# Decoder layer on one core: later key stacks by a ScalarE copy and GpSimd head products, rope partly on GpSimd, two head groups per output bank

## The chip, the cores and the metric

One core of a Trainium2 chip runs the whole kernel. The metric is the device time of one execution in microseconds. TensorE does the matmuls (its records are called PE, its weight loads PEld), VectorE is DVE, ScalarE is ACT, GpSimd is POOL, and SyncE (SP) issues DMAs.

## What is computed

A decoder layer with the norms behind the residuals, for x of 2 x 512 x 128 and a context of 2 x 154 x 128, all in fp32:

```python
x = layernorm(x + self_attention(x))       # 16 heads of 8; causal
x = layernorm(x + cross_attention(x, ctx)) # 16 heads of 8; keys 154
x = layernorm(x + ffn(x))                  # 8 experts of 256, the best 2 of each token

# self attention
q = rope(x @ wq.T); k = rope(x @ wk.T); v = rope(x @ wv.T)
qh, kh, vh = q @ wqi.T + bqi, k @ wki.T + bki, v @ wvi.T + bvi
attn = softmax(where(causal, qh @ kh.T / sqrt(8), -inf))
out = (attn @ vh) @ out_w.T + out_b
```

The ffn is silu(h1) * h3 through w2 for every expert, weighted by the router.

## The kernel before

The layout is transposed: channels on the 128 partitions, 512 tokens in the free dimension. The 16 heads go in NG = 4 groups of G = 4, one head to each 32 partitions. A **unit** u is one stage (0 self, 1 cross), one batch and one group: NU = 16 units, of which the first 8 are self attention.

The steps, by the names that the planner's items have:

- `U` (b, w), w one of q, k, v: x times wq, wk or wv (L748), then VectorE multiplies the bank by the cosine and the sine table into `ab` (L1142, L1144). That is the rope; its swap of neighbours is in the weights of the next step.
- `H` (b, w): projection of q or k by four fp32 records (L755, L756). ScalarE rounds it to `high` (L990), VectorE writes the rest to `low` (L1150). `VH` is the same for v (L766), written to `v_sb` (L1183), which has 32 columns for each head: 8 of v, a one for the sum, zeros.
- `SQ`, `SK` (b, g): 0/1 matrices `fr` select a group's rows from high and low into one bank (L725, L726), so that each head's 32 partitions hold the parts of q or k. `fr` is made by ScalarE from loaded constants (`FR`, L980 four times and L981). ScalarE copies q to `qa`. The key **stack** `kst` of a unit has a block of 512 columns for each head and zeros on the other heads' partitions: ScalarE writes the blocks of heads 0 and 1 (L1010, 32 partitions each), VectorE those of heads 2 and 3 (L1165), into tiles that were cleared at the start. `SC` does so for the context's keys, `kc` (L1018, L1173).
- `A` (u, k): scores by query rows (L812), 11 banks a unit in self attention, 6 in cross attention. VectorE takes the negative row maximum of each head (L1230, L1235).
- `MP` (u): GpSimd writes the 16 maxima, rounded, and their rests to `mpad` (L666, L667). `MT` (u): TensorE adds them to q by a matmul with the identity (L822, L824); ScalarE copies the result to `qb`.
- `B` (u, k): scores by key rows (L840), ScalarE's Exp to `prob` (heads 0, 1) and `prob_more` (L1047). `MK`: GpSimd zeroes above the diagonal (L675, two instructions for each of four key tiles).
- `PV` (u, kt): v times probabilities, four heads at once, each on 32 columns of the array (L857; in cross attention L865, L868). The key tiles 0, 1, 3, 2 are items of their own.
- `POC` (u): ScalarE copies the output bank `psO`, of which there is one, so PV of unit u + 1 waits for it. `OT` (u): four transposes (L876), VectorE divides by the sums (L1246, L1247). After four groups `ONT`, `OP` (output projection), `LN`, `LNX`.
- `XB`: GpSimd adds a bias to the loaded x_tok (L638). `F1`, `F3`, `F2`: the experts (L719 to L721, L947), two loops of 16 tiles.

PSUM's eight banks are rings: `psA` 3, `psB` 2, `psO` 1, `psJ` 2 for everything else (`J`). All engines run fixed lists of items in the order that `schedule` writes: a list scheduler over `tasks()`, which gives every item its stages (engine, microseconds), the items it waits for, and rings. It starts what can start first, and among equals what has the longest way to the end. At run time each engine goes through its list in order and waits on semaphores.

Loads are issued at the start by SP and by ScalarE, one (`brow`, the bias rows) by GpSimd.

Of the kernel before, what the change touches and what calls it, by code (L numbers as in the profile page):

```python
# [43 lines left out]
C_CQ = C_ONE + 4  # L44
# [13 lines left out]

SIZE = {"A": 3, "B": 2, "O": 1, "J": 2}
Y_AFTER = (NU - NG - 2 if SIZE["O"] == 2 else NU - 1, NU - 1)  # L60
# [42 lines left out]
def po_bank(u):  # L103
    return u % 2 if u < NU - NG and SIZE["O"] == 2 else SIZE["O"] - 1


def po_back(u):

    return 2 if u < NU - NG and SIZE["O"] == 2 else 1
# [9 lines left out]

def part_users(n):  # L120

    key = [k for k, v in PART.items() if v == n][0]
    if key == ("c",):
        return [("SC", (g,)) for g in range(NG)]
    if key[0] == "k":
        return [("SK", (key[1], g)) for g in range(NG)]
    return [("SQ", (int(key[0] == "x"), key[1], g)) for g in range(NG)]
# [4 lines left out]
    "J": {"U": (1, 1), "H": (1, 2), "VH": (1, 1), "SQ": (1, 1), "SK": (1, (1, 2)), "SC": (1, (1, 2)), "CK": (2, 1), "CV": (1, 1),  # L132
# [5 lines left out]
LATENCY = {"PE": 0.22, "ACT": 0.17, "DVE": 0.15, "POOL": 0.18, "SP": 0.1, "LOAD": 0.1}  # L138


def tasks():
# [16 lines left out]
    dve = lambda n: 0.065 + n / 958.0  # L158
    act = lambda n: 0.12 + n / 1390.0
    mm = lambda n: max(0.137, n / 2300.0)  # L160
# [3 lines left out]
    add("LOAD", (0,), [("LOAD", 6.5)])  # L164
    add("LOAD", (1,), [("LOAD", 1.0)])
    add("LOAD", (2,), [("LOAD", 1.5)])
    add("LOAD", (3,), [("LOAD", 6.0)])
    add("FR", (), [("ACT", 2.4)], [("LOAD", (2,))])
    for b in range(B):
        for n, w in enumerate("qkv"):  # L170
            late = []
            if 3 * b + n >= 2:
                m = 3 * b + n - 2
                late.append((1, ((("H", (m // 3, "qk"[m % 3])) if m % 3 < 2 else ("VH", (m // 3,))), 0)))
            add("U", (b, w), [("PE", 0.86), ("DVE", 1.2)], [("LOAD", (b,))], late)
# [21 lines left out]
    for u in range(NU):  # L197
        st, b, g = unit(u)
        fills = a_fills(u)
        for k, parts in enumerate(fills):  # L200
# [3 lines left out]
            deps = [("SQ", (st, b, g)), ("SK", (b, g)) if st == 0 else ("SC", (g,))] if k == 0 else []  # L204
# [4 lines left out]
        add("MP", (u,), [("POOL", 0.5)], [("A", (u, len(fills) - 1))] + ([(("MT", (u - 2,)), 0)] if u >= 2 else []))  # L209
        add("MT", (u,), [("PE", 0.78), ("ACT", 0.5)], [("MP", (u,))],  # L210
            [(1, (("B", (u - 2, len(b_fills(u - 2)) - 1)), 0))] if u >= 2 else [])
        for k, blocks in enumerate(b_fills(u)):
            widths = [S - 128 * kt if st == 0 else S for kt, _, _ in blocks]
            deps = [("MT", (u,))] + ([("KT", ())] if st == 1 and k == NG else [])
            late = [(1, ("PV", (u - 2, 2 if unit(u - 2)[0] == 0 else 1)))] if u >= 2 and k == 0 else []
            add("B", (u, k), [("PE", sum(mm(w) for w in widths)), ("ACT", act(sum(widths)))], deps, late)
        if st == 0:
            for kt in (0, 1, 3, 2):
                add("MK", (u, kt), [("POOL", 0.72)], [("B", (u, exps_of(u, kt)[-1]))])
            pv = [(kt, us, [("MK", (u, kt)), ("VH", (b,))]) for kt, us in ((0, 0.86), (1, 0.65), (3, 0.22), (2, 0.43))]  # L220
# [1201 lines left out]
```

## Time and profile before

| | us |
|---|---|
| runs | 289.09, 289.03, 287.84; median 289.03 |
| the profiled execution | 290.4 |
| its span, first to last instruction | 288.3 |
| PE, DVE, ACT, POOL busy | 262.7, 203.1, 155.9, 110.8 |
| mean granted TensorE clock | 0.975 |

The span is about 2 us shorter than the execution's own time. "Busy" is the time that an engine's instructions cover. Matmuls overlap and their ends are modelled, so a stretch in which PE is always busy can still hold small waits. Clock 1.00 is 2.4 GHz, 0.50 is 1.2 GHz.

### The profile page before, as it was taken

The page shows a single profiled execution, that of the slowest core. Times are in us where ns is not written, and L with a number is a line of the kernel's source. Part 1 is how long each engine was busy: PE and PEld are TensorE (multiplying, and loading weights), DVE is VectorE, ACT ScalarE, POOL GpSimd, SP SyncE. Part 2 cuts the span into 40 slices and gives each one's busy share as a digit, 9 for nine tenths or more (in the row PEclk, how much of TensorE's full clock was granted, in tenths as well). Part 3 has the DMA queues.
Part 4 walks back from the last instruction along what each step waited for, and adds up shares of the span by engine and source line. Part 5 has one row for each costly group of instructions (what it writes and reads, how often), then busy time and mean ns, then how long its engine had stood idle before and what let it go on. Part 6 is the DMA issues. An engine that isn't in the chain of part 4 may idle for free.

```text
span 288.3 us, 4324 instructions
## 1 busy us (share of the span) xinstructions
PE 262.7 (91%) x1326; PEld 161.2 (56%) x1326; DVE 203.1 (70%) x603; ACT 155.9 (54%) x293; POOL 110.8 (38%) x175
## 2 busy tenths in 40 slices
PE   6478799999999899999999989999989999999980
PEld 2135656655655556667654666566656556565640
DVE  7639688897889988766573499835788854555464
ACT  1446135576789955867788747685342333432300
POOL 9950003413323353133743232025364455554531
PEclk9977799999999999999999999999999999999997
DMA  7920002000000400000212100000000000000002
GB/s 199 392 60 0 1 0 75 0 3 1 3 0 0 145 3 0 2 1 0 68 44 67 45 1 0 2 1 0 2 0 1 0 2 0 0 0 2 0 0 73
DMA packets 5797, 8.62 MB, mean 30 GB/s; under 512 B 720, under 2 KB 3280, under 8 KB 5648
## 3 DMA queue, kind: packets, MB, share of 16 engines
q1 hardware_dynamic: 4976, 7.14, 7.6%
q10 hardware_dynamic: 720, 0.95, 0.9%
q0 software_dynamic: 80, 0.26, 0.6%
q8 instruction: 11, 0.18, 0.3%
q14 instruction: 10, 0.08, 0.1%
HBM read 7.83 MB, written 0.52 MB: 29 GB/s over the span
## 4 chain that ended last, share of the span: by engine, by line
PE 76%; ACT 7%; DVE 7%; issue 3%; DMA 3%; POOL 2%; SPq 0%; POOLq 0%; DVEq 0%; ACTq 0%
PE psB L840 10%; PE psA L812 10%; PE psO L947 8%; PE psO L857 7%; PE psB L719 3%; PE psO L865 3%; DMA c<-c_dram 3%; PE psJ L876 2%; PE psO L868 2%; PE psA L720 2%; PE psA L721 2%; PE psA L719 2%; PE psB L721 2%; PE psB L720 2%; PE psJ L824 2%
## 5 line engine op out<-in xcount | busy, mean ns | idle before, releaser
L1230 DVE CUSTOM_DVE_ANT_0 junk<-psA,c 128x128 bf16<-128x128 f32 (+3 forms) x128 | 56.1, 486 | 5.8 <-PE psA L812 5.4
L690 POOL TENSOR_TENSOR gated<-silu,wbc 128x512 f32<-128x512 f32 x32 | 41.1, 1286 | 41.5 <-DVE hid L1344 30.1
L1047 ACT ACTIVATE prob<-psB 128x512 f32<-128x512 f32 (+1 forms) x88 | 47.6, 560 | 16.1 <-PE psB L840 15.0
L1101 ACT ACTIVATE silu<-psA 128x512 f32<-128x512 f32 x32 | 19.1, 598 | 44.6 <-PE psA L721 40.3
L1334 DVE SCALAR_TENSOR_TENSOR silu<-silu,psA 128x512 f32<-128x512 f32 x32 | 21.9, 684 | 27.8 <-ACT silu L1101 27.8
L812 PE MATMUL psA<-kst,qa 128*128 128x512 f32 (+1 forms) x88 | 39.8, 460 | 1.3 <-DVE kst L1165 1.2
L840 PE MATMUL psB<-qb,kst 128*128 128x512 f32 (+3 forms) x128 | 37.6, 337 | 1.0 <-ACT prob_more L1047 0.5
L1235 DVE TENSOR_REDUCE negm<-psA 128x3 f32<-128x462 f32 (+1 forms) x48 | 26.1, 579 | 10.3 <-PE psA L812 9.9
L947 PE MATMUL psO<-hid,w 128*128 128x512 f32 x64 | 33.1, 598 | 0.2 <-DVE hid L1344 0.2
L675 POOL TENSOR_SCALAR_AFFINE_SELECT prob<-prob 128x256 f32<-128x256 f32 x32 | 13.2, 413 | 50.3 <-ACT prob_more L1047 50.1
L1047 ACT ACTIVATE prob_more<-psB 128x512 f32<-128x512 f32 (+1 forms) x48 | 24.6, 530 | 12.1 <-PE psB L840 11.6
L840 PEld LDWEIGHTS psB<-qb,kst 128*128 128x128 f32 x128 | 22.6, 189 | 12.3 <-issue 5.2
L812 PEld LDWEIGHTS psA<-kst,qa 128*128 128x128 f32 x88 | 17.1, 195 | 15.8 <-issue 11.4
L1344 DVE TENSOR_TENSOR hid<-psB,gated 128x512 f32<-128x512 f32 x32 | 21.9, 686 | 3.4 <-PE psB L721 3.2
L857 PE MATMUL psO<-prob,v 128*32 128x512 f32 (+3 forms) x128 | 23.4, 445 | 1.0 <-POOL prob_more L675 1.0
L857 PE MATMUL psO<-prob_more,v 128*32 128x512 f32 (+3 forms) x128 | 23.4, 445 | 0.0
L719 PE MATMUL psA<-x_high,w1high 128*128 128x512 f32 x32 | 22.0, 687 | 0.0
L666 POOL CAST mpad<-negm 128x16 fp32r<-128x16 f32 x16 | 3.4, 212 | 44.0 <-DVE negm L1230 26.2
L812 PE MATMUL psA<-kc,qa 128*128 128x462 f32 (+2 forms) x64 | 18.5, 345 | 0.3 <-DVE negm L1235 0.2
L840 PE MATMUL psB<-qb,kc 128*128 128x512 f32 x32 | 15.6, 498 | 1.3 <-ACT prob L1047 0.9
L719 PE MATMUL psB<-x_high,w3high 128*128 128x512 f32 x32 | 16.5, 515 | 0.0
L725 PE MATMUL psJ<-high,fr 128*128 128x512 f32 (+1 forms) x28 | 13.0, 465 | 3.4 <-DVE kst L1165 2.1
(150 smaller groups left out, 522.9 us busy)
## 6 DMA issues: line engine op xcount, KB each, us to landing
c<-w_dram SPq DMA_DIRECT2D x8, 256.0 KB, 2.8
w<-w_dram SPq DMA_DIRECT2D x1, 1024.0 KB, 4.9
c<-c_dram SPq DMA_DIRECT2D x1, 666.0 KB, 9.4
xT<-xt_dram SPq DMA_DIRECT2D x2, 256.0 KB, 6.0
x_tok<-x_dram SPq DMA_DIRECT2D x1, 512.0 KB, 10.0
out_dram<-x_tok SPq DMA_DIRECT2D x2, 256.0 KB, 2.3
wa<-wa_dram ACTq DMA_DIRECT2D x2, 192.0 KB, 5.5
wx<-wx_dram SPq DMA_DIRECT2D x1, 384.0 KB, 8.6
```

The costliest lines, as they stand in the source:

```text
L690: nc.gpsimd.tensor_tensor(gated[:, n % 2, :], silu[:, n % 2, :], wbc[:, (E * b + f // 2) % 2, :], ALU.mult).then_inc(s_sg, 1)
L719: nc.tensor.matmul(ps[:, :], w_high[:, cols], x_high[:, b, :], start=True, stop=False)
L812: last = nc.tensor.matmul(ps[:, c:c + heads * width].rearrange("p (n w) -> p n w", n=heads), qa[:, u % SLOTS, 128 * i:128 * i + 128], keys ...
L840: last = nc.tensor.matmul(ps[:, c:c + S - 128 * kt], keys, qb[:, u % 2, 128 * kt:S], start=m == 0, stop=m == len(blocks) - 1, skip_group_c ...
L857: last = nc.tensor.matmul(po[32 * j:32 * j + 32, 128 * kt:S], v_sb[b][:, kt, G * g + j, :], prob_at(u, kt, j), start=kt == 0, stop=kt == 2 ...
L947: nc.tensor.matmul(psO[b % SIZE["O"]][:, :], w2[:, 128 * f:128 * f + 128], hid[:, n % 4, :], start=f == 0, stop=f == FT - 1).then_inc(s_y, 1)
L1047: nc.scalar.activation(dst, psB[n % SIZE["B"]][:, 0:cols], ACT.Exp, scale=SCALE).then_inc(b_done[n % SIZE["B"]], 1)
L1101: nc.scalar.activation(silu[:, n % 2, :], psA[a % SIZE["A"]][:, :], ACT.Tanh, scale=0.5).then_inc(s_th, 1)
L1230: last = nc.vector.tensor_tensor_reduce(out=junk[:, p, cols], in0=psA[p][:, cols], in1=c32[:, C_MASK + S - width:C_MASK + S], scale=-1.0, ...
L1235: last = nc.vector.tensor_reduce(negm[:, u % 2, :, :].rearrange("p i j -> p (i j)")[:, G * i + j:G * i + j + heads], psA[p][:, 0:heads * S ...
L1334: nc.vector.scalar_tensor_tensor(out=silu[:, n % 2, :], in0=silu[:, n % 2, :], scalar=1.0, in1=psA[a % SIZE["A"]][:, :], op0=ALU.add, op1= ...
L1344: nc.vector.tensor_tensor(hid[:, n % 4, :], psB[h % SIZE["B"]][:, :], gated[:, n % 2, :], ALU.mult).then_inc(b_done[h % SIZE["B"]], 1)
```

## The change

1. **Stacks.** Only unit 0 keeps the old way (now `SK0`). For the other seven, ScalarE copies the whole bank with its bias to a new tile `kcomp` (two buffers), which frees the bank, and GpSimd writes the four blocks of `kst`, each a product of kcomp over 128 partitions with a column `C_HEAD + j` that is 1 on head j's partitions and 0 elsewhere. Zeros are then written with the rest, so three of the four kst buffers and kc are no longer cleared. `SC` goes the same way (308 columns).
2. **Rope** of (0, v) and of batch 1: ScalarE copies the bank to `rest`, GpSimd makes both products. (0, q) and (0, k) stay on VectorE.
3. **MP** goes from GpSimd to VectorE, same two instructions.
4. **Output bank.** Units of even and odd g share one bank: v's 8 columns and the one now start at column 16 of each 32, and a group reads a window of 32 columns that begins at 16 (even g) or 0 (odd g), so that its results fall into the lower or upper half and zeros into the other. `POC` and `OT` are done once for two units, 8 times instead of 16.
5. **Bursts.** The PV items of self attention are two instead of four: key tile 0, then 1, 3 and 2 together.
6. **Loads and first items.** On SP: `wa` 7:10, `brow` and `c16` come in (c16 last), the selection constants go to ScalarE's queue. `FR` is five items, and a selection waits for its own group alone. U (0, v) waits for H (0, k), U of batch 1 for MT (0).
7. `onorm` lies in the constants' memory. The planner's latencies and costs have other numbers, which moves items on every engine.

```diff
+BURSTS = ((0,), (1, 3, 2)), ((0,), (1,))
+ROPE = {(b, w): "DVE" if (b, w) in ((0, "q"), (0, "k")) else "POOL" for b in range(B) for w in "qkv"}
+V_AT = 16
+def v_from(g):
+    return V_AT * (1 - g % 2)
...
-LATENCY = {"PE": 0.22, "ACT": 0.17, "DVE": 0.15, "POOL": 0.18, "SP": 0.1, "LOAD": 0.1}
+LATENCY = {"PE": 0.21, "ACT": 0.2, "DVE": 0.18, "POOL": 0.16, "SP": 0.1, "LOAD": 0.1}
...
+            if (b, w) == (0, "v"):
+                deps.append((("H", (0, "k")), 0))
+            if b:
+                deps.append((("MT", (0,)), 0))
...
-            act.dma_start(wa[:, 7:10, :], wa_d[:, 7:10, :]).then_inc(s_iv, 16)
-            act.dma_start(c16[:, :], c16_d).then_inc(s_c16, 16)
+            act.dma_start(c32[:, C_FR:C_MASK], c32_d[:, C_FR:C_MASK]).then_inc(s_fr, 16)
...
+                elif kind == "U":
...
+                    nc.gpsimd.tensor_tensor(ab[:, n % 2, 0, :], rest[:, m % 2, :], c32[:, C_CA:C_CA + S], ALU.mult)
+                    nc.gpsimd.tensor_tensor(ab[:, n % 2, 1, :], rest[:, m % 2, :], c32[:, C_SA:C_SA + S], ALU.mult).then_inc(s_rope, 1)
+                elif kind == "SK":
...
+                    for j in range(G):
+                        nc.gpsimd.tensor_scalar(kst[:, u % SLOTS, j, :], kcomp[:, u % 2, :], c32[:, C_HEAD + j:C_HEAD + j + 1], None,
+                                                ALU.mult).then_inc(s_km, 1)
...
-                    for j in (0, 1):
-                        rows = slice(32 * j, 32 * j + 32)
-                        last = nc.scalar.activation(kst[rows, u % SLOTS, j, :], ps[rows, :], ACT.Identity, bias=c32[rows, C_ONE:C_ONE + 1])
-                    free(JOB[item], last)
+                    if u >= 3:
+                        act.wait_ge(s_km, G * (u - 2))
+                    free(JOB[item], nc.scalar.activation(kcomp[:, u % 2, :], ps[:, :], ACT.Identity, bias=c32[:, C_ONE:C_ONE + 1]))
...
+                            for j in range(G):
+                                last = nc.tensor.matmul(psO[32 * j:32 * j + 32, 128 * kt:S], v_window(v, g, j), prob_at(u, kt, j),
+                                                        start=kt == 0 and g % 2 == 0, stop=st == 0 and kt == 2 and g % 2 == 1,
+                                                        skip_group_check=True)
...
-                    act.wait_ge(s_pv, u + 1)
-                    if u >= 2:
-                        job_done(act, "OT", u - 2)
-                    nc.scalar.activation(po_sb[:, u % 2, :], psO[po_bank(u)][:, :], ACT.Copy).then_inc(s_po, 1)
+                    act.wait_ge(s_pv, 2 * p + 2)
+                    if p:
+                        job_filled(act, ("OT", (p - 1,)))
+                    nc.scalar.activation(po_sb[:, :], psO[:, :], ACT.Copy).then_inc(s_po, 1)
```

**Where items move.** TensorE from its first matmul after the warm-up to the first score fill, before (L748 is U, L755 and L756 are H, L725 and L726 a selection, L812 is A):

```order
L748 MATMUL psJ0<-xT,wa 128x512
L748 MATMUL psJ1<-xT,wa 128x512
L755 MATMUL psJ0<-ab,wa 128x512
L756 MATMUL psJ0<-ab,wa 128x512
L748 MATMUL psJ1<-xT,wa 128x512
L755 MATMUL psJ0<-ab,wa 128x512
L756 MATMUL psJ0<-ab,wa 128x512
L725 MATMUL psJ1<-high,fr 128x512
L726 MATMUL psJ1<-low,fr 128x512
```

and of the change (L808 is U, L815 and L816 are H, L785 and L786 a selection):

```order
L808 MATMUL psJ0<-xT,wa 128x512
L808 MATMUL psJ1<-xT,wa 128x512
L815 MATMUL psJ0<-ab,wa 128x512
L816 MATMUL psJ0<-ab,wa 128x512
L815 MATMUL psJ1<-ab,wa 128x512
L816 MATMUL psJ1<-ab,wa 128x512
L785 MATMUL psJ0<-high,fr 128x512
L786 MATMUL psJ0<-low,fr 128x512
```

The third U, of v, no longer stands between the projections of q and k, and k's goes to the other bank.

TensorE ahead of the first `MT`, before (L766 is VH, L822 and L824 are MT); eleven fills of unit 0 and one of unit 1 are done by then:

```order
L766 MATMUL psJ0<-wa,ab 128x128 x8
L812 MATMUL psA2<-kst,qa 128x512
L748 MATMUL psJ1<-xT,wa 128x512
L812 MATMUL psA0<-kst,qa 128x512
L755 MATMUL psJ0<-ab,wa 128x512
L756 MATMUL psJ0<-ab,wa 128x512
L812 MATMUL psA1<-kst,qa 128x512
L755 MATMUL psJ1<-ab,wa 128x512
L756 MATMUL psJ1<-ab,wa 128x512
L812 MATMUL psA2<-kst,qa 128x512
L822 MATMUL psJ0<-qa,fr_id 128x512
L824 MATMUL psJ0<-fr_id,mpad 128x128 x4
```

and of the change (L876 is A, L826 is VH, L887 and L889 are MT); fourteen fills are done by then:

```order
L876 MATMUL psA1<-kst,qa 128x512
L876 MATMUL psA2<-kst,qa 128x512
L826 MATMUL psJ1<-wa,ab 128x128 x8
L876 MATMUL psA0<-kst,qa 128x512
L876 MATMUL psA1<-kst,qa 128x512
L887 MATMUL psJ0<-qa,fr_id 128x512
L889 MATMUL psJ0<-fr_id,mpad 128x128 x4
```

Both U (L748, the second earlier in the list) and both H of batch 1 have left the place ahead of `MT`; VH stays ahead of it.

GpSimd after its clearings, before (L666, L667 are MP, L675 is MK, L643, L644 clear tiles):

```order
L638 TENSOR_TENSOR x_tok<-x_tok,brow 128x1024
L666 CAST mpad<-negm 128x16
L667 TENSOR_TENSOR mpad<-negm,mpad 128x16
L675 AFFINE_SELECT prob<-prob 128x2x128
L675 AFFINE_SELECT prob_more<-prob_more 128x2x128
L643 MEMSET kt_sb 128x1024
```

and of the change (L714 are stack products, L703, L704 a rope, L735 is MK):

```order
L682 TENSOR_TENSOR x_tok<-x_tok,brow 128x1024
L714 TENSOR_SCALAR kst<-kcomp,c32 128x512 x4
L703 TENSOR_TENSOR ab<-rest,c32 128x512
L704 TENSOR_TENSOR ab<-rest,c32 128x512
L714 TENSOR_SCALAR kst<-kcomp,c32 128x512 x8
L703 TENSOR_TENSOR ab<-rest,c32 128x512
L704 TENSOR_TENSOR ab<-rest,c32 128x512
L735 AFFINE_SELECT prob<-prob 128x2x128
L735 AFFINE_SELECT prob_more<-prob_more 128x2x128
```

Three stacks and two ropes now stand between XB and the first mask, the v rope behind the stack of unit 1.

## Rows read from the trace of the kernel before

**Rows 1.** The page: span, engines, slices of TensorE, and the row maxima's group.

```profile
span 288.3 us, 4324 instructions
...
PE 262.7 (91%) x1326; PEld 161.2 (56%) x1326; DVE 203.1 (70%) x603; ACT 155.9 (54%) x293; POOL 110.8 (38%) x175
...
PE   6478799999999899999999989999989999999980
...
L1230 DVE CUSTOM_DVE_ANT_0 junk<-psA,c 128x128 bf16<-128x128 f32 (+3 forms) x128 | 56.1, 486 | 5.8 <-PE psA L812 5.4
```

**Rows 2.** Windows: length, PE, PEld, DVE, ACT, POOL busy, clock, DMA share, GB/s.

```profile
0.00:40.10 40.10, 28.82 (x80) 15.80 (x81) 27.21 (x57) 13.87 (x21) 17.74 (x19) 0.87 0.36 117
40.10:276.00 235.90, 229.91 (x1236) 143.70 (x1235) 169.31 (x520) 141.48 (x271) 90.57 (x152) 1.00 0.05 14
14.70:18.10 3.40, 3.29 (x5) 1.03 (x4) 0.13 (x1) 0.76 (x2) 2.31 (x2) 0.50 0.41 100
84.00:96.00 12.00, 9.91 (x71) 6.09 (x70) 11.57 (x39) 11.53 (x24) 4.87 (x14) 1.00 0.00 0
```

**Rows 3.** The chain of waits from 2 to 24 us: start, length, what.

```profile
2.17 7.38 DMA c<-c_dram
...
12.18 0.31 ACT fr_id L981
...
21.27 0.58 PE psA L812
```

**Rows 4.** Timeline of the start: start, length, instruction, idle before.

```profile
8.82 1.10 PE L755 MATMUL psJ<-ab,wa 128*128 128x512 f32 x2 [2.49 <-DMA bcol<-bcol_dram]
...
16.80 2.35 POOL L638 TENSOR_TENSOR x_tok<-x_tok,brow 128x1024 f32<-128x1024 f32 x1 [1.09 <-DMA x_tok<-x_dram]
...
40.29 0.39 PE L822 MATMUL psJ<-qa,fr_id 128*128 128x512 f32 x1
```

**Rows 5.** Groups by shape: count, busy us and mean ns, idle before.

```profile
L690 POOL TENSOR_TENSOR gated<-silu,wbc 128x512 f32<-128x512 f32 x32 | 41.1, 1286 | 41.5 <-DVE hid L1344 30.1 <-DVE silu L1334 11.2
L675 POOL TENSOR_SCALAR_AFFINE_SELECT prob<-prob 128x256 f32<-128x256 f32 x32 | 13.2, 413 | 50.3 <-ACT prob_more L1047 50.1
L654 POOL CAST kt_sb<-kc 32x208 fp32r<-32x208 f32 x4 | 1.4, 354 | 2.0 <-ACT kc L1018 1.8
L666 POOL CAST mpad<-negm 128x16 fp32r<-128x16 f32 x16 | 3.4, 212 | 44.0 <-DVE negm L1230 26.2 <-DVE negm L1235 15.7 <-PE psJ L883 2.0
...
L1165 DVE TENSOR_SCALAR kst<-psJ,c 32x512 fp32r<-32x512 f32 x16 | 12.1, 753 | 3.3 <-PE psJ L726 3.1
L1144 DVE TENSOR_TENSOR ab<-psJ,c 128x512 f32<-128x512 f32 x6 | 4.1, 680 | 0.0
L1246 DVE RECIPROCAL rec<-psJ 128x16 f32<-128x16 f32 x16 | 4.1, 256 | 4.9 <-PE psJ L876 4.8
L1010 ACT ACTIVATE kst<-psJ,c 32x512 fp32r<-32x512 f32 x16 | 10.9, 679 | 4.7 <-PE psJ L726 4.4
```

**Rows 6.** The chain: v's projection at either clock, and one OT group.

```profile
31.58 3.60 PE psJ L766 x16
...
46.43 1.84 PE psJ L766 x16
...
60.14 0.44 PE psJ L876 x4
```

**Rows 7.** Timeline of TensorE around a PV burst of 128 columns.

```profile
53.53 0.28 PE L840 MATMUL psB<-qb,kst 128*128 128x256 f32 x1
53.74 0.30 PE L857 MATMUL psO<-prob,v 128*32 128x128 f32 x2
...
54.09 0.44 PE L812 MATMUL psA<-kst,qa 128*128 128x384 f32 x1
```

**Rows 8.** Window of GpSimd alone: length, busy, clock, DMA share, GB/s.

```profile
16.80:110.00 93.20, 25.83 (x67) 0.96 0.05 18
```

**Rows 9.** Waits of the whole span: us in total, times, longest.

```profile
ACT prob L1047 <- PE psB L840: 15.0, 24, 1.5
```

More of the change, by code:

```diff
@@ L43 @@
 C_ONE = C_MASK + S
-C_CQ = C_ONE + 4
+C_HEAD = C_ONE + 4
+C_CQ = C_HEAD + G
 C_SQ = C_CQ + S
@@ L100, in exps_of, with last_pv @@
     return {0: range(4), 1: [4]}[kt]
[L103 to L109, printed above, removed]
+BURSTS = ((0,), (1, 3, 2)), ((0,), (1,))
[3 more added lines that the diff above has]
+    return V_AT * (1 - g % 2)
+def last_pv(u):
+    return ("PV", (u, len(BURSTS[unit(u)[0]]) - 1))
 def masks(u, kt):
@@ L214, in tasks @@
             deps = [("MT", (u,))] + ([("KT", ())] if st == 1 and k == NG else [])
-            late = [(1, ("PV", (u - 2, 2 if unit(u - 2)[0] == 0 else 1)))] if u >= 2 and k == 0 else []
+            late = [(1, last_pv(u - 2))] if u >= 2 and k == 0 else []
             add("B", (u, k), [("PE", sum(mm(w) for w in widths)), ("ACT", act(sum(widths)))], deps, late)
@@ L378, in freed_counts @@
             place = len(counts) % SIZE["J"]
-            last[place] += 2 if item[0] in ("SK", "SC") else 1
+            last[place] += 2 if item[0] == "SK0" else 1
             counts.append(last[place])
@@ L571, in prob_at, with roped, v_window @@
             return prob[:, u % 2, n * S:(n + 1) * S]
+        def roped(eng, b, w):
+            if ROPE[b, w] == "DVE":
+                job_done(eng, "U", b, w)
+            else:
+                eng.wait_ge(s_rope, ROPED.index(("U", (b, w))) + 1)
+        def v_window(tile, g, j):
+            first = 32 * (G * g + j) + v_from(g)
+            return tile[:, first:first + 32]
         def parts_made(eng, n):
@@ L851, in _ @@
                             job_done(pe, "CV")
-                        if u >= po_back(u):
-                            pe.wait_ge(s_po, u - po_back(u) + 1)
-                    if st == 0:
-                        pe.wait_ge(s_mk, masks(u, kt))
-                        for j in range(G):
-                            last = nc.tensor.matmul(po[32 * j:32 * j + 32, 128 * kt:S], v_sb[b][:, kt, G * g + j, :],
-                                                    prob_at(u, kt, j), start=kt == 0, stop=kt == 2, skip_group_check=True)
-                        if kt == 2:
-                            last.then_inc(s_pv, 1)
-                    else:
-                        fill_done(pe, "B", [("B", (u, k)) for k in exps_of(u, kt)])
-                        if kt == 0:
+                        if g % 2 == 0 and u:
+                            pe.wait_ge(s_po, u // 2)
```

313 lines of the change are left out of this document (180 added, 133 removed).

## The prediction

> **What bounds the kernel now.** I read the page first, then the windows, then the chain of waits and the timeline of the start. The page gives TensorE 91% of a 288.3 us span, VectorE 70%, ScalarE 54%, GpSimd 38% [rows 1]. The slices say more: TensorE is at eight or nine tenths from the sixth slice to the last but two, and below that in the first five. The windows put numbers to it [rows 2]: in the first 40.1 us TensorE is busy for 28.8 us, and part of that is at half clock (0.50 in 14.7:18.1, so 1.2 GHz). From 40.1 to 276 it is busy 229.9 of 235.9 us. So two things can shorten the run: an earlier start of the dense part, and less for TensorE to do in it. Relief of other engines pays only where TensorE idles or waits under its modelled ends.
>
> The chain of the start [rows 3] runs so. The transfer of the selection matrices lands at 9.55. ScalarE then copies all five pieces of them, until 12.49, before `high` of q, which stood behind them. VectorE's `low` takes until 14; only then does TensorE begin the projection of k, which waits for a bank, since the third rope product had taken the other. `high`, `low`, the selection and the first stack follow, and the first score fill starts at 21.27. From there VectorE sets the pace: it reads 16 maxima of unit 0 and between them writes its half of three more stacks, and two ropes. TensorE starts the first `MT` at 40.29 [rows 4].
>
> **Start, new order.** Loads first. SP's queue gets `wa` 7:10, `brow` and, last, `c16`, and gives the selections to ScalarE's; GpSimd's and ScalarE's queues lose `brow` and `c16`, so 0.54 MB leaves the front. I leave all landings where they are (x_tok is one place later on SP, but `c16` no longer comes before it). VectorE's and GpSimd's dropped clearings gain nothing: the q projection waits for bcol's load until 8.82 anyway [rows 4], and GpSimd for x_tok's. The projection takes 4 records of 0.43, to 10.6. One selection copy (a fifth of what now ends at 12.49, 0.63) is over by 10.3, so `high` runs 10.8 to 11.5 and `low` to 12.3. The k projection needs no third bank and follows q directly, 10.6 to 12.3. ScalarE makes two more copies, so `high` of k is 12.8 to 13.5, `low` to 14.3, the selection (0.47 + 0.25) to 15.1, the stack (0.75 + 0.77) to 16.7. First score fill: 16.8 against 21.27.
>
> The 128 tiles of maxima keep VectorE busy for 56.1 us [rows 1], 7.0 a unit, so unit 0 is read from 17.5 to 24.5. Before `MT` TensorE must still do the v projection, and that hangs on GpSimd: x_tok lands and is worked off from 16.80 to 19.15 [rows 4]; behind it stand four products of stack 1, then the rope of v. Rope is two products of two tensors at 1.286 [rows 5], 2.6 us.
>
> **The price p of one stack product** (one tensor, 128x512, scalar per row) is in no row. Below: the one-input CAST, 212 ns at 16 elements and 354 at 208, 0.74 ns each, gives 0.58 us at 512 [rows 5]. The mask, one input at 256 elements, takes 0.413, doubled 0.83. Above: two tensors, 1.286. I take 0.75, nearest the mask less its fixed part. A page states less: by the Trainium skill, "GPSIMD Engine Reference", section 3.1, a body of one input moves an element in 1.03 cycles, which is an estimate of 0.44 us plus dispatch; by that the start would gain 1 us more. The same page of the Trainium skill (section 4.1) advises VectorE for elementwise work, since two inputs run about half as fast on GpSimd; the rope rows agree (1.286 on GpSimd against 0.680 on VectorE [rows 5]), and rival 3 below is what that rule would make of this change.
>
> So stack 1 is ready at 22.2, rope v at 24.7, the v projection (1.84 at full clock, 3.60 at half [rows 6]) at 26.6 to 28.4, two fills more, `MT` at 27.1 to 28.9. I take 28.0, 12.3 us earlier than 40.29. Not all is gain: before `MT` the old order had done two U products (0.86 each) and both projections of batch 1 (1.72 each) that now come later, 5.2 us, while two score fills (0.22 each) now come ahead. **Start: -12.3 + 4.7 = -7.6 us.** Bounds: -4.5 if the v projection meets half clock and p is 1.29; -10 if loads come 1 us sooner and p is 0.58.
>
> **Two groups per output bank.** TensorE loses 8 of 16 `OT` groups of transposes, 0.44 each [rows 6]: **-3.5 us**, all on TensorE's own time. ScalarE loses 8 copies of a bank, VectorE 8 reciprocals. The windowed v of 32 columns costs TensorE the same as before. Units of even g now wait for the copy where each unit did, so no wait is added. Bounds -3.0 and -4.0.
>
> **Bursts.** The probability products of tiles 1, 3, 2 now run together, 16 entries and exits of the 32-column form less. In [rows 7] the 256-column B at 53.53 needs 0.107 us (its columns at 2.4 GHz) and the burst starts 0.21 later; the 128-column burst needs 0.21 and is followed after 0.35: 0.10 in, 0.14 out, 3.8 us for 16. Where TensorE waits anyway it is nothing. I take **-2.5 us**, bounds 0 and -3.8.
>
> **Relief and new waits.** VectorE loses 14 half stack writes (0.753), 8 narrower ones of kc (about 0.5) and 4 ropes (twice 0.680), 20 us, and gets 16 MP pairs. I price each of the two at the small reciprocal's 0.256 [rows 5], 8 us in all: hidden beside TensorE, and 0.5 us a unit in `MT`'s way if that cover goes. ScalarE writes one copy where it wrote two halves (0.679) in seven stacks and four kc groups, some 7 us less, and trades 8 output copies for 4 of rope. From 84 to 96 VectorE was busy 11.57 and ScalarE 11.53 of 12 us, TensorE 9.91 [rows 2]: that 2.1 us should return. GpSimd: from 16.8 to 110 it was busy 25.8 us [rows 8]. Now less 7 MP pairs (0.45), plus 4 ropes (2.57), plus 28p, plus 16 kc products of 308 columns at 0.68p: 33 + 38.9p, which is 62 us at p = 0.75, in some 81 us (the same stretch, 12 shorter). Not the bound, but in-order: masks stand behind 3 us of products, which the probability products then wait for. I take -2 and +1: **-1 us**, bounds -6 and +9.
>
> Projections, cross attention's matmuls, the experts (203 to 276) and the last 12.3 us keep their work; the later weight loads have 90 us to spare. The planner's altered costs move items among equals: nothing, bounds -1 and +2.
>
> **Sum**: 288.3 - 7.6 - 3.5 - 2.5 - 1 = 273.7 us of span; this execution took 290.4, 2.1 above its span, and lay 1.4 above the median of 289.03. Forecast: 273.7 + 2.1 - 1.4 = **274.4 us**.
>
> **Rivals.** (1) *The attention was held by VectorE and ScalarE more than TensorE's busy time shows.* For it: the ends of matmuls are modelled, psB has only two banks, and one half of the probabilities alone waits 15.0 us for B [rows 9]. Against: TensorE waits little by its own records. Then relief is -8 instead of -1: 267 us.
> (2) *GpSimd gives part back.* p = 1.29 fills it: 33 + 50 = 83 of 81 us. Start 2 worse, masks late by 4 x 0.54 behind each of seven stacks, of which I count half, 7 more: 283 us. For it: the gated product shows 1.286. Against: that row reads two tensors.
> (3) *GpSimd becomes the bound, slower than before.* If a product with a scalar per row costs 1.6 us or more, 33 + 38.9 x 1.6 = 95 us, 14 over; with some 5 for stacks that come late to their score fills, 274.4 + 19 = 293 us. It decides from p = 1.6 on. For it: no row has this operation at this size. Against: the one-input rows lie at half of 1.6 or less, and even two tensors stay under it.
> (4) *Nothing reaches the end*: the early score fills only queue up behind the probabilities and the projections of batch 1 come as late as before. 288 us. Against: TensorE had no idle time after 40 in which the saved work could vanish.
>
> **Chances.** Forecast 0.53 (271 to 278), rival 1 0.17, rival 2 0.16, rival 3 0.09, rival 4 0.05. A measurement can tell about 0.5% (1.4 us) from no change. Faster: 0.53 + 0.17 + 0.16 = 0.86; same 0.05; slower 0.09. The range takes in rivals 1 and 2: 266 to 286 us.
>
> **What the new profile would show.** First score fill near 17 and first MT near 28; 32 output transposes instead of 64; p as a row of its own on GpSimd, 0.6 to 0.85 us; GpSimd busy 60 us by 100; the first F2 some 14 us before 203.7. Wrong would be: p over 1.2, TensorE waiting for stacks or masks by more than 3 us in all, an x_tok load that lands after 19, or a dense part that is longer than before less 6 us.

## The result, and the profile after

The changed kernel took **303.72 us** (median; 301.0 to 305.2) against 289.06 (287.84 to 290.25) for the kernel before: a ratio of 1.050, 95% interval 1.041 to 1.058. It is slower by 5%; the forecast was 274.4, range 266 to 286. The profiled execution took 303.75 us with a span of 302.0. Medians here and below take in every run, while the ratios leave out runs over 1.5% above the fastest of their kernel; without those, three medians below would be 290.17 in place of 291.12, 279.89 in place of 280.50 and 276.03 in place of 277.68.

The page of the kernel after, beside [rows 1]: span, busy time by engine, slices of PE and POOL and of TensorE's clock, the shares of the last chain, and groups.

```profile
span 302.0 us, 4259 instructions
...
PE 261.6 (87%) x1294; PEld 162.0 (54%) x1294; DVE 195.6 (65%) x596; ACT 145.6 (48%) x278; POOL 164.7 (55%) x191
...
PE   6685968888889696699999987999999999999980
...
POOL 8089992839796999813163431003455365555441
PEclk9996979979999899689999999999999999999997
...
PE 62%; POOL 22%; issue 5%; ACT 4%; DVE 3%; DMA 1%; POOLq 0%; ACTq 0%; DVEq 0%
...
L714 POOL TENSOR_SCALAR kst<-kcomp,c 128x512 fp32r<-128x512 f32 x28 | 43.3, 1569 | 5.5 <-PE psB L905 4.1
...
L735 POOL TENSOR_SCALAR_AFFINE_SELECT prob<-prob 128x256 f32<-128x256 f32 x32 | 13.1, 410 | 30.4 <-ACT prob_more L1121 30.3
...
L720 POOL TENSOR_SCALAR kc<-kcomp,c 128x308 fp32r<-128x308 f32 x16 | 16.6, 1062 | 0.0
```

The row that no trace of before had is L714: **a product costs 1.569 us**, not 0.75, and one of kc 1.062. GpSimd, 2% of the chain that ended last before, is 22% of it now, and TensorE 62% in place of 76%. Only GpSimd is busy for a larger share (55% against 38%); TensorE falls from 91% to 87%, VectorE from 70% to 65%, ScalarE from 54% to 48%. These three have no more work than before, in a longer span.

The windows of the kernel after, columns as in [rows 2]:

```profile
0.00:40.10 40.10, 29.65 (x103) 18.09 (x103) 27.09 (x86) 18.12 (x30) 30.70 (x28) 0.91 0.36 118
40.10:276.00 235.90, 214.04 (x1131) 133.67 (x1132) 154.62 (x474) 123.58 (x242) 124.65 (x155) 0.96 0.05 14
16.80:110.00 93.20, 76.19 (x428) 49.74 (x426) 63.42 (x245) 44.59 (x88) 75.53 (x84) 0.91 0.05 18
24.90:31.70 6.80, 5.07 (x21) 4.48 (x21) 3.08 (x12) 0.33 (x1) 6.80 (x6) 0.52 0.00 1
41.90:45.40 3.50, 3.50 (x5) 1.39 (x5) 3.50 (x1) 0.00 (x1) 3.50 (x6) 0.56 0.00 0
```

From 40.1 to 276 TensorE was busy 229.9 us before [rows 2] and is 214.0 now: it is busy for 16 us less of that stretch. GpSimd, 25.8 us of 16.8:110 before [rows 8], now has 75.5. In 24.9:31.7, after TensorE had waited for a stack, and in 41.9:45.4, behind a wait for rope, its granted clock is 0.52 and 0.56, near the lower of its two levels (0.50, 1.2 GHz): both of these idle stretches are followed by work at half speed.

Who waits for whom, over the span (us in total, times, longest):

```profile
PE psO L928 <- POOL prob_more L735: 13.4, 7, 3.0
PE psJ L826 <- POOL ab L704: 3.0, 2, 1.7
PE psA L876 <- POOL kst L714: 2.5, 1, 2.5
PE psJ L815 <- POOL ab L704: 2.5, 1, 2.5
```

The probability products wait 13.4 us for GpSimd's masks; it was 1.0 us before. Projections wait for rope behind products, 5.5 us, and a score fill 2.5 for stack 1. The timeline shows the place (start, length, instruction):

```profile
15.43 0.47 PE L876 MATMUL psA<-kst,qa 128*128 128x512 f32 x1 [1.24 <-DVE kst L1232]
15.87 2.39 POOL L682 TENSOR_TENSOR x_tok<-x_tok,brow 128x1024 f32<-128x1024 f32 x1 [8.63 <-DMA x_tok<-x_dram]
...
18.24 6.21 POOL L714 TENSOR_SCALAR kst<-kcomp,c 128x512 fp32r<-128x512 f32 x4
...
24.55 0.77 PE L876 MATMUL psA<-kst,qa 128*128 128x512 f32 x1 [2.48 <-POOL kst L714]
...
25.64 1.26 POOL L704 TENSOR_TENSOR ab<-rest,c 128x512 f32<-128x512 f32 x1
26.88 6.19 POOL L714 TENSOR_SCALAR kst<-kcomp,c 128x512 fp32r<-128x512 f32 x4
27.05 3.75 PE L826 MATMUL psJ<-wa,ab 128*128 128x128 f32 x16 [1.73 <-POOL ab L704]
...
31.42 0.39 PE L887 MATMUL psJ<-qa,fr_id 128*128 128x512 f32 x1
```

The first score fill is early, at 15.43. Then comes 6.21 us for stack 1 where I had 3.0, rope v until 26.9, v's projection at half clock (3.75, and 1.84 at full [rows 6]), and the first `MT` at 31.42.

### The profile page after: what moved, and what is told of

Its sections match the earlier page's. It is cut to its first block, busy times and chain, and to the rows that moved or that the text cites. A ratio compares the mean times of both kernels' runs of the same rounds, so it can differ in the third digit from the quotient of the medians.

```text
span 302.0 us, 4259 instructions
## 1 busy us (share of the span) xinstructions
PE 261.6 (87%) x1294; PEld 162.0 (54%) x1294; DVE 195.6 (65%) x596; ACT 145.6 (48%) x278; POOL 164.7 (55%) x191
## 4 chain that ended last, share of the span: by engine, by line
PE 62%; POOL 22%; issue 5%; ACT 4%; DVE 3%; DMA 1%; POOLq 0%; ACTq 0%; DVEq 0%
POOL kst L714 12%; PE psO L1014 9%; PE psO L928 7%; PE psB L905 6%; POOL kc L720 5%; PE psA L876 5%; PE psB L779 3%; PE psA L780 2%; PE psB L780 2%; PE psA L781 2%; PE psB L781 2%; PE psA L779 2%; PE psO L933 2%; PE psJ L993 2%; DMA c<-c_dram 1%
## 5 line engine op out<-in xcount | busy, mean ns | idle before, releaser
L714 POOL TENSOR_SCALAR kst<-kcomp,c 128x512 fp32r<-128x512 f32 x28 | 43.3, 1569 | 5.5 <-PE psB L905 4.1
L876 PE MATMUL psA<-kst,qa 128*128 128x512 f32 (+1 forms) x88 | 39.0, 453 | 4.0 <-POOL kst L714 2.5
L905 PE MATMUL psB<-qb,kst 128*128 128x512 f32 (+3 forms) x128 | 40.5, 360 | 0.5 <-ACT prob_more L1121 0.2
L928 PE MATMUL psO<-prob,v 128*32 128x512 f32 (+3 forms) x128 | 22.9, 466 | 13.5 <-POOL prob_more L735 13.4
L905 PEld LDWEIGHTS psB<-qb,kst 128*128 128x128 f32 x128 | 23.7, 199 | 17.1 <-issue 9.5
L735 POOL TENSOR_SCALAR_AFFINE_SELECT prob<-prob 128x256 f32<-128x256 f32 x32 | 13.1, 410 | 30.4 <-ACT prob_more L1121 30.3
L876 PEld LDWEIGHTS psA<-kst,qa 128*128 128x128 f32 x88 | 18.1, 207 | 11.4 <-issue 7.9
L779 PE MATMUL psA<-x_high,w1high 128*128 128x512 f32 x32 | 22.8, 712 | 0.0
L876 PE MATMUL psA<-kc,qa 128*128 128x462 f32 (+2 forms) x64 | 18.2, 335 | 1.6 <-DVE negm L1306 1.5
L1106 ACT ACTIVATE qb<-psJ 128x512 fp32r<-128x512 f32 x16 | 9.6, 598 | 16.6 <-PE psJ L889 16.2
L928 PEld LDWEIGHTS psO<-prob,v 128*32 128x32 f32 x128 | 5.6, 110 | 21.5 <-POOL prob_more L735 16.0
L720 POOL TENSOR_SCALAR kc<-kcomp,c 128x308 fp32r<-128x308 f32 x16 | 16.6, 1062 | 0.0
```

Source lines behind the costliest of these rows:

```text
L714: nc.gpsimd.tensor_scalar(kst[:, u % SLOTS, j, :], kcomp[:, u % 2, :], c32[:, C_HEAD + j:C_HEAD + j + 1], None, ALU.mult).then_inc(s_km, 1)
L720: nc.gpsimd.tensor_scalar(kc[:, :, g, j, :], kcomp[:, g % 2, 0:B * SC].rearrange("p (b t) -> p b t", b=B), c32[:, C_HEAD + j:C_HEAD + j + ...
L779: nc.tensor.matmul(ps[:, :], w_high[:, cols], x_high[:, b, :], start=True, stop=False)
L876: last = nc.tensor.matmul(ps[:, c:c + heads * width].rearrange("p (n w) -> p n w", n=heads), qa[:, u % SLOTS, 128 * i:128 * i + 128], keys ...
L905: last = nc.tensor.matmul(ps[:, c:c + S - 128 * kt], keys, qb[:, u % 2, 128 * kt:S], start=m == 0, stop=m == len(blocks) - 1, skip_group_c ...
L928: last = nc.tensor.matmul(psO[32 * j:32 * j + 32, 128 * kt:S], v_window(v, g, j), prob_at(u, kt, j), start=kt == 0 and g % 2 == 0, stop=st ...
```

## The experiments

Two theories. **The price**: a product costs too much, GpSimd is in the way of masks, ropes and stacks, and the rest of the change is worth what I forecast. **The rivals**: the order that the planner made, the work moved to VectorE, or a contention at SBUF is what costs.

**Copies in place of products.** Every item stays in the same order on every engine; GpSimd writes each head's 32 rows with a copy into a cleared stack, and waits for each. The clearing of the stacks and of kc at the start comes back with it, on GpSimd and VectorE. The cut shows the main lines.

```
-    nc.gpsimd.tensor_scalar(kst[:, u % SLOTS, j, :], kcomp[:, u % 2, :], c32[:, C_HEAD + j:...], None, ALU.mult)
+    nc.gpsimd.tensor_copy(kst[rows, u % SLOTS, j, :], kcomp[rows, u % 2, :]).then_inc(s_km, 1)
+    pool.wait_ge(s_km, G * (u - 1) + j + 1)
```

> The change, every engine's list of items as it is, but GpSimd writes a stack as four copies of 32 partitions (the tiles are cleared at the start as before, and it waits for each copy) instead of four products over 128. Theory A, the price of the product (1.57 us instead of the 0.75 that I took) made GpSimd the bound of self attention: a copy costs about 0.6 us with its wait 0.7, GpSimd has 24 us less of stacks and 8 less of kc, and the run takes 274 to 282 us. Theory B, the order of items, the MP on VectorE that waited 7.8 us beside GpSimd's work, or the shared bank made the loss: it stays above 292.

Measured: **275.34 us** (272.46 to 276.05), ratio 0.953, interval 0.949 to 0.957. Of this kernel's page:

```profile
span 270.7 us, 4270 instructions
...
PE   7669999999999999999998799999999999999970
...
PE 83%; ACT 5%; DVE 4%; issue 3%; POOL 2%; DMA 2%; POOLq 0%; ACTq 0%; DVEq 0%
```

Its groups by shape and its windows (the same columns as above):

```profile
L729 POOL CAST kst<-kcomp 32x512 fp32r<-32x512 f32 x28 | 17.1, 612 | 6.5 <-PE psB L925 3.1 <-ACT kcomp L1106 1.4 <-POOL x_tok L693 0.2
```

```profile
16.80:110.00 93.20, 91.47 (x587) 61.32 (x588) 75.77 (x318) 60.91 (x123) 60.37 (x117) 1.00 0.05 18
```

With 0.61 us a head GpSimd is back at 2% of the chain, TensorE's clock is 1.00 in this window, and TensorE is busy 91.5 of those 93.2 us in place of 76.2. The choice of one GpSimd operation decides between 4.7% faster and 5% slower. The first `MT` starts at 26.52:

```profile
26.52 0.47 PE L907 MATMUL psJ<-qa,fr_id 128*128 128x512 f32 x1
```

**The maxima's pair back on GpSimd**, in the change as it is. I had seen one VectorE copy there take 7.78 us (below).

```
-    add("MP", (u,), [("DVE", 0.4)], ...
+    add("MP", (u,), [("POOL", 0.5)], ...
```

> The change with MP back on GpSimd, nothing else (the planner moves some items with it). Theory A (price of the products): VectorE's 7.8 us CAST at 38 us disappears, but stacks still set the pace, 298 to 304 us. Theory B (VectorE's small SBUF instructions starve beside GpSimd's): 285 to 293 us.

Measured: 304.59 us (304.04 to 305.9), ratio 1.054 (1.050 to 1.059), no better than the change. **The same edit on the kernel with copies:**

> The copies of e1_copy and MP back on GpSimd together. Theory A alone: within 2 us of e1_copy. If MP on VectorE starves and that reaches the end once GpSimd is no longer the bound: 4 to 8 us below e1_copy, 268 to 276.

Measured: 274.04 us (273.18 to 275.61), ratio 0.950 (0.945 to 0.954), level with the copies alone. Where this pair stands decides nothing measurable, so the 7.78 us are not the cause of the loss.

**Stacks by ScalarE and VectorE in halves**, as before, the rest of the change kept.

> The change with stacks and kc written as before, halves on ScalarE and VectorE, tiles cleared; rope, MP, shared output bank, bursts, loads and first items stay changed. Theory A: without the products the rest is a gain, 274 to 283 us. Theory B (order, MP or shared bank at fault): above 289.

Measured: 281.08 us (280.21 to 281.31), ratio 0.972 (0.968 to 0.976). So stacks on GpSimd pay at the right price: 6 us less than halves by copies, 23 more by products. In the profiled executions the first `MT` starts at 31.71 with halves, 5.2 us behind that of the copies, so most of the 6 us is there already at the start:

```profile
31.71 0.47 PE L874 MATMUL psJ<-qa,fr_id 128*128 128x512 f32 x1
```

**A constant in place of the heads' column** in the product (the heads' masks are left out).

```
-    ... kcomp[:, u % 2, :], c32[:, C_HEAD + j:C_HEAD + j + 1], None, ALU.mult)
+    ... kcomp[:, u % 2, :], 0.25, None, ALU.mult)
```

> The change as it is, same order of items, but the 28 products of the stacks and the 16 of kc multiply by the constant 0.25 in place of the column with one number per row (so all four blocks of a stack are alike and no head is masked: the scores lose their heads' separation). Theory A (the second, per-row operand is what costs: a GpSimd instruction with a scalar per row reads it like a second input): the product of 128x512 falls from 1.57 us to between 0.55 and 0.80, GpSimd is busy under 45 us in 16:110 in place of 76, and the time comes near that of the four copies, 274 to 280 us. Theory B (GpSimd's multiply with rounding to the short float form is slow whatever the operand): it stays at 1.4 to 1.6 us and the time at 302 to 305 us.

Measured, in a single run: 294.0 us, the product at 1.493. The theory that the number per row is what costs falls: a constant saves 0.08 us. That the time still fell by some 10 us, for 3 us less of GpSimd's work, rests on that single run, fits neither expectation, and stays open. In 16.8:110 GpSimd was busy 80.1 us there and TensorE 80.5.

**The planner told the true price** (6.3 us a stack, 4.3 for kc); same work, other order.

> The change with the planner told 6.3 us for a stack of products (four of 1.57) in place of 3.0 and 4.3 for kc in place of 2.0: no work added or removed, only the order differs. Theory A (GpSimd has too much work in the first 110 us: 76 us of busy time in 94, whatever the order): 296 to 303 us, still slower than before, the masks' waits shorter. Theory B (the planner's wrong price made an order in which masks stand behind products; with the right one the loss goes): 280 to 288 us.

Measured: 291.12 us (288.45 to 295.11), ratio 1.005 (1.000 to 1.009), between the two expectations. Order alone gives back 12.6 of the 14.7 us that the change loses (13.6 by the median of 290.17). TensorE hardly waits for masks any more:

```profile
PE psO L928 <- POOL prob_more L735: 0.8, 2, 0.5
```

and its window shows GpSimd filled better, 84.1 us against 75.5, with TensorE at 86.9 against 76.2:

```profile
16.80:110.00 93.20, 86.92 (x499) 56.40 (x501) 73.90 (x305) 53.02 (x107) 84.14 (x95) 0.98 0.05 18
```

**Each copy made twice**, and **half of them twice**, in the order of the copies, those of kc too: a dose of GpSimd work and of nothing else.

```
+    link(nc.gpsimd.tensor_copy(kst[rows, u % SLOTS, j, :], kcomp[rows, u % 2, :]))
     nc.gpsimd.tensor_copy(kst[rows, u % SLOTS, j, :], kcomp[rows, u % 2, :]).then_inc(s_km, 1)
```

> The four copies of 32 partitions in place of products (275.3 us, 0.61 us a copy), but every copy made twice, in the same order of items: a head costs some 1.25 to 1.35 us of GpSimd instead of 0.61, which is the 1.29 of my second rival; about 20 us more of GpSimd's busy time before 140. Theory A (the loss is a matter of GpSimd's load near its limit: nothing is lost while it has room, everything beyond it is): 283 to 292 us, and TensorE's waits for masks return. Theory B (a load on GpSimd as such is harmless, and the product costs by something else it does, such as holding up VectorE at the shared port): within 3 us of 275.3.

> Copies for products, the first two of the four heads' copies made twice: a head costs GpSimd 0.92 us on average, between the 0.61 of single copies (275.3 us) and the 1.22 of double ones (294.6 us). Theory A (the loss grows evenly with what a head costs): 283 to 287 us. Theory B (there is a point of saturation, free below it): 275 to 280 us.

Measured: 294.56 us (293.4 to 296.65), ratio 1.023 (1.015 to 1.031), and 282.39 us (280.56 to 283.37), ratio 0.978 (0.973 to 0.984). A stack occupies GpSimd, first start to last end, for 2.62 us with single copies, 3.95 with half of them double, 5.30 with all double and 6.2 with products; the times are 275.3, 282.4, 294.6 and 303.7. The first dose cost slightly less and the second more than I had expected. There is no free part: the first 1.3 us a stack cost 7 us, the next 1.3 cost 12, the last 0.9 cost 9. Interpolated between half and all double, the line of no change (289) is crossed near 4.7 us a stack, 1.2 a head, in this order of items. TensorE's waits for masks return with the dose, 4.0 us in all with half of the copies double and 9.0 with all:

```profile
PE psO L951 <- POOL prob_more L758: 9.0, 7, 3.3
```

The windows of 16.8:110, all double first, then half:

```profile
16.80:110.00 93.20, 78.00 (x479) 51.56 (x479) 68.13 (x283) 49.22 (x98) 73.69 (x136) 0.97 0.06 18
```

```profile
16.80:110.00 93.20, 86.00 (x524) 57.31 (x524) 73.46 (x304) 54.57 (x110) 70.52 (x135) 0.98 0.06 18
```

From half double to all double to products GpSimd's busy time in the window hardly rises (70.5, 73.7, 75.5), TensorE's falls (86.0, 78.0, 76.2). GpSimd is never filled: over the whole span it waits 30.3 us for exponentials before its masks in the kernel after, and ScalarE's exponentials wait 40.6 us for TensorE's fills. Its share of 0.81 is no fixed ceiling, though: with the constant, in the same order, it was 0.86, and with the planner told the true price 0.90.

**Prices alone.** The change as it is, and behind GpSimd's last item three of each form, alone; then the stream of the start beside small VectorE copies.

> The change as it is, and behind GpSimd's last item a row of instructions of its own, three of each form, each waiting for the one before, while no other engine computes: the product of 128x512 with a number per row (into the short float form), with a constant, into plain f32, at 256 columns, on 32 partitions; a copy of 128x512 and of 32x512; a product of two tensors, the second the column of the heads broadcast or a real tensor; an affine select of 512 columns. Then the stream of the start twice over (four products, four tensor products, four selects, back to back) beside small VectorE copies of maxima (128x16, 0.18 us by themselves). The added work lies behind the last item, so the total time says nothing. Theory A (the product with a scalar is slow as an operation of GpSimd, alone or in company): 1.5 to 1.6 us for 128x512 with column or constant, about half at 256 columns, and the product of two tensors is cheaper at 1.28. Theory B (1.57 us is contention in the kernel): alone it takes 0.6 to 0.9 us. For the small copy, theory C (VectorE is kept out by a back-to-back stream of GpSimd): single copies of over 2 us beside the stream. Theory D (what held it was one event of the kernel, not the stream): none above 1 us.

The groups of that part (the window of this view holds one of the three products of the first form):

```profile
L764 POOL TENSOR_SCALAR kst<-kcomp,c 128x512 fp32r<-128x512 f32 x1 | 1.6, 1564 | 0.1
L766 POOL TENSOR_SCALAR kst<-kcomp 128x512 fp32r<-128x512 f32 x3 | 4.5, 1490 | 0.3
L768 POOL TENSOR_SCALAR gated<-kcomp,c 128x512 f32<-128x512 f32 x3 | 4.7, 1565 | 0.3
L770 POOL TENSOR_SCALAR kst<-kcomp,c 128x256 fp32r<-128x256 f32 x3 | 2.8, 924 | 0.3
L772 POOL TENSOR_SCALAR kst<-kcomp,c 32x512 fp32r<-32x512 f32 x3 | 4.7, 1554 | 0.3
L774 POOL CAST kst<-kcomp 128x512 fp32r<-128x512 f32 x3 | 1.8, 615 | 0.2
L776 POOL CAST kst<-kcomp 32x512 fp32r<-32x512 f32 x3 | 1.8, 606 | 0.2
L778 POOL TENSOR_TENSOR kst<-kcomp,c 128x512 fp32r<-128x512 f32 x3 | 3.1, 1040 | 0.2
L780 POOL TENSOR_TENSOR kst<-kcomp 128x512 fp32r<-128x512 f32 x3 | 3.8, 1262 | 0.2
L782 POOL TENSOR_SCALAR_AFFINE_SELECT gated<-kcomp 128x512 f32<-128x512 f32 x3 | 1.8, 614 | 0.2
```

The 1.56 us are the operation's own, in company or not, whatever the output's type or the number of partitions (32 rows cost 1.55); a constant in place of the column takes 1.49. A copy and a select of the same shape take 0.61. And **the same product written with two tensors**, the second the column broadcast along the row, takes 1.04.

**That form in the change.** One expression, same result, same order:

```
-    nc.gpsimd.tensor_scalar(kst[:, u % SLOTS, j, :], kcomp[:, u % 2, :], c32[:, C_HEAD + j:C_HEAD + j + 1], None, ALU.mult)
+    nc.gpsimd.tensor_tensor(kst[:, u % SLOTS, j, :], kcomp[:, u % 2, :],
+                            c32[:, C_HEAD + j:C_HEAD + j + 1].to_broadcast([128, S]), ALU.mult)
```

> The change as it is, in its own order, with each product written as a product of two tensors, the second of them the heads' column broadcast along the row: by itself 1.04 us in place of 1.56. Same result, no copies by block. 28 x 0.53 and 16 x about 0.35 us less on GpSimd, 20 us. Theory A (what a head costs GpSimd sets the time; 0.92 gave 282.4 and 1.22 gave 294.6): between those, 286 to 290 us, the same as before. Theory B (contention: two-tensor instructions hold VectorE's small copy for 1.19 us instead of 0.63, so little is won): 293 to 300 us.

> The same, and the planner told 4.2 us for a stack and 2.8 for kc. Telling it the true price returned 12.6 us at 1.57 a product. Theory A (order and price add up): 279 to 284 us. Theory B (with 20 us less of work the order's share is mostly gone already): 284 to 288 us.

Measured: **280.50 us** (278.04 to 282.23), ratio 0.973 (0.967 to 0.978); with the planner told 4.2 and 2.8 us: 277.68 us (275.79 to 280.15), ratio 0.964 (0.957 to 0.970). Both are faster than I expected. I had interpolated over the price of a head. The time of a stack is the better measure, since no waits stand between the four: 4.05 us, beside 3.95 for half double, would give 283 by the doses. The order's share shrinks from 12.6 to some 3 us, which is near the noise. The run also speaks against a contention at SBUF as the cause: this form holds VectorE's small copies longer than the product with a scalar does (0.93 against 0.43 us, last section), and yet the kernel is no slower than copies of the same length. The groups of the first of the two, on GpSimd:

```profile
L714 POOL TENSOR_TENSOR kst<-kcomp,c 128x512 fp32r<-128x512 f32 x28 | 28.5, 1058 | 4.7 <-PE psB L905 3.2 <-ACT kcomp L1086 1.4
...
L720 POOL TENSOR_TENSOR kc<-kcomp,c 128x308 fp32r<-128x308 f32 x16 | 10.7, 703 | 0.0
```

**The rest of the change, on the kernel with copies.** All ropes on VectorE; that with the maxima's pair on GpSimd; four items of probability products a unit in place of the burst; that with the pair on GpSimd; and the output transposes issued twice, as many as before.

> The kernel with copies (275.3 us), and all six ropes on VectorE as before, in the order that the planner then makes. ScalarE loses four copies of a bank, GpSimd 8 products of two tensors (1.27 us, 10 us in all), VectorE gains 8 instructions of 0.68 (5.4 us). Theory A (moving rope was worth nothing once GpSimd has the stacks: v's projection waits for it at the start): 271 to 275 us. Theory B (VectorE is the scarcer of the two in the first 110 us): 276 to 280 us.

> Copies for products, the maxima's pair on GpSimd as before and all ropes on VectorE as before: what is left of the change is the order of loads and first items, ScalarE's copy plus GpSimd's block copies, the bursts and the shared output bank. Theory A (both moves of small work were worth nothing or less): 272 to 275 us, at or below the 274.0 and 275.7 of the kernels with one of them undone. Theory B (VectorE needs the relief): 276 to 280 us.

> Copies for products, and the probability products in four items a unit as before in place of two (tile 0; tiles 1, 3, 2 together); the planner makes its order anew. Theory A (an entry and an exit of the 32-column form cost TensorE 0.24 us, 16 of them or more, and TensorE bounds this kernel): 277.5 to 279.5 us, 2 to 4 above 275.3. Theory B (TensorE has room, or the finer items let it fill its waits): 273 to 276 us.

> Copies for products, the maxima's pair on GpSimd and four items of probability products a unit: the two single edits that measured 274.0 and 274.4 us, together. Theory A (they add): 272.5 to 274 us. Theory B (each was only the scatter of the planner's orders): 274 to 276 us.

> Copies for products, same order, with every transpose of the 8 output groups issued twice, the second over the first: 8 x 4 more transposes on TensorE, which is the number that the shared output bank took away (0.44 us a group by the trace of before, 3.5 in all). Theory A (they stand on TensorE's own time at full price): 278 to 279.5 us. Theory B (the group lies partly in gaps): 275.5 to 277.5 us.

| on the kernel with copies, 275.34 us | us (range) | ratio (interval) |
|---|---|---|
| ropes on VectorE | 275.66 (275.53 to 276.49) | 0.956 (0.950 to 0.962) |
| ropes on VectorE, pair on GpSimd | 275.91 (275.23 to 276.69) | 0.954 (0.950 to 0.958) |
| four items for the bursts | 274.37 (274.19 to 275.24) | 0.950 (0.945 to 0.955) |
| four items, pair on GpSimd | 273.73 (272.87 to 274.56) | 0.947 (0.944 to 0.951) |
| output transposes twice | 276.39 (276.06 to 278.13) | 0.958 (0.952 to 0.963) |

None of the five differs from the copies by more than the intervals allow. So moving rope or the pair is worth nothing that these runs can tell, and neither are the bursts. The 32 transposes put back add 3.5 us to their group's busy time (8.4 in place of 4.9) and 1.05 us to the median, with intervals wide enough for 0 to 3 us. The profiled executions lie further apart: the first of the experts' matmuls starts 3.4 us later with the transposes twice (the copies first):

```profile
174.82 0.39 PE L799 MATMUL psA<-x_high,w1high 128*128 128x512 f32 x1
```

```profile
178.26 0.40 PE L799 MATMUL psA<-x_high,w1high 128*128 128x512 f32 x1
```

But the profiled execution of the copies is the fastest of its four, 2.9 us below their median, so these runs do not settle what the transposes cost. The version with four items and the pair on GpSimd has the lowest median here, and beats both kernels.

## Why the prediction was wrong

*The price p of one stack product* is the step that failed. I took 0.75 us between 0.58 and 1.286; it is 1.569. The upper bound was no bound: it took for granted that an operation with one input and a scalar can't cost more than one with two tensors. Alone they measure 1.564 and 1.262. The rows I leaned on, copy and mask, are a different price: 0.61 at the same shape. The Trainium skill's "GPSIMD Engine Reference", section 3.1, would have led to the same error: its rate of 1.03 cycles an element without a second input is an estimate of 0.44 us plus dispatch, which the copy (0.615 us) bears out and the product does not, and section 4.1 calls one input "roughly line-rate". Section 4.1's advice to keep elementwise work on VectorE would have warned of this change, but the copies show stacks on GpSimd 6 us better than in halves.

*The mechanism is that of rival 3*, to which I gave 0.09: GpSimd in the way, slower. But its condition was mis-sized as well. I had it decide from 1.6 us, where 95 us of work would overfill 81. In the same order of items the runs put the point near 1.2, and lose 7 us already at 0.92: rival 2, which counted 9 us at p = 1.29, was too mild in the same way, since copies of 1.22 measured 294.6 where it said 283. The step that failed with the price is the comparison of GpSimd's work with the length of the stretch, as if nothing were lost until it is full. By my own sum, 33 + 38.9p, the copies half double make 69 us and all double 80 us of 81, and these cost 7 and 19 us over single copies. GpSimd waits for ScalarE between its items, so what is added is late for someone long before it is full. My 1 us for masks behind 3 us of products was 13.4 us of waits behind 6.2. The planner's costs (3.0 for a stack) made it worse: telling it 6.3 gives back 12.6 us, where I had costed the planner's figures at -1 to +2.

*Start*: forecast -7.6. With the product, first `MT` at 31.42: -8.9 + 4.7 = -4.2, just beyond my bound of -4.5, and for the reasons named there (half clock in v's projection, a dear product). With copies it is 26.52: -13.8 + 4.7 = -9.1, 1.5 better than forecast. The first score fill came 1.4 earlier than forecast in the kernel after, since q's projection starts at 7.2 and not at 8.8: it waits for the rope and no longer for bcol's load. So I was wrong that the dropped clearings gain nothing. With copies, where VectorE clears a second stack before the rope again, q's projection starts at 8.62 and the first score fill at 16.82, as forecast.

*Shared output bank*: forecast -3.5; the transposes put back cost 1 us by the medians and 3.4 between the two profiled executions. Whether the term was too large stays open. The copies of ScalarE and reciprocals saved with it were not tested.

*Bursts*: forecast -2.5; measured on the kernel with copies, nothing (274.4 with four items, 275.3 with two). That is the bound of 0.

*Relief*: forecast -1 with a spread up to -8 in rival 1. Moving rope and the pair is worth nothing that shows. Stacks off ScalarE and VectorE are worth 6 us, 281.1 with halves against 275.3 with copies; but 5.2 us of that stands at the first `MT` already and belongs to the start. For rival 1's relief of the dense part that leaves under 1 us by the medians and 3.4 by the two profiled executions (281.1 and 272.5).

*Sum*: no run has a product of 0.75. The copies cost 0.61 a head and took 275.3, where I said 274.4, and between the doses a stack of 3.0 us comes to 277, an estimate; the range would have held. The agreement is partly luck: the bursts gave nothing of their 2.5 us, and the start gave 1.5 more than its term.

## What to carry to other kernels

A price that no row shows has no upper bound from a "harder-looking" neighbour: measure the exact form once, alone, before moving 44 of it to another engine, and try its other spellings, as one expression was worth 23 us here. Do not compare an in-order engine's load with the length of the stretch alone: it waits between its items, and here the first 1.3 us added to a stack already cost 7. Where a planner sets the order, give it the measured price: the wrong one cost some 13 us here, about what the change lost.

## What the hardware showed that was not expected

GpSimd's product of a tensor and a scalar (1.56 us for 512 columns, 0.92 for 256) is slower than its product of two tensors (1.26), and much slower than a copy or a select (0.61); a broadcast second tensor is cheaper (1.04) than a real one. The number of partitions does not matter (32 against 128: 1.554 and 1.564 for the product, 0.606 and 0.615 for the copy).

Small VectorE copies stand still beside it. In the kernel after, one of 128x16, elsewhere 0.18 us, took 7.78 us while GpSimd worked without a break (the last product, rope, masks, rope, masks):

```profile
38.55 7.78 DVE L1243 CAST mpad<-negm 128x16 fp32r<-128x16 f32 x1
...
39.19 1.27 POOL L703 TENSOR_TENSOR ab<-rest,c 128x512 f32<-128x512 f32 x1
...
44.81 0.41 POOL L735 TENSOR_SCALAR_AFFINE_SELECT prob<-prob 128x256 f32<-128x256 f32 x1
```

In the kernel of prices, windows with that copy alone (length, busy, clock, DMA share, GB/s), beside products of a scalar, beside products of two tensors, and with GpSimd at rest:

```profile
332.30:337.80 5.50, 5.12 (x12) 0.50 0.01 1
337.90:342.70 4.80, 4.66 (x5) 0.50 0.00 0
...
360.00:370.00 10.00, 8.41 (x47) 0.50 0.00 0
```

That is 0.43, 0.93 and 0.18 us a copy. The longest there was 1.2 us, so neither stream made 7.78; what did is open. The Trainium skill, "GPSIMD Engine Reference", section 1, says that the two engines share SBUF interfaces, with contention for VectorE instructions in a 2-port mode or with two SBUF inputs. The slower copies beside GpSimd fit that if they ran in such a mode, which no row shows.
